# Mixes of a recurrent layer: one fp32 matmul in place of three matmuls of split parts

## The reference

```
xx  = shift(x) - x
xxx = x + xx * time_maa_x
m   = tanh(xxx @ time_maa_w1).reshape(b, t, 4, 32)
m   = einsum('btfd,fdc->fbtc', m, time_maa_w2)      # mw, mk, mv, mr: the four mixes
xw  = x + xx * (time_maa_w + mw)                    # xk, xv, xr alike
r, k, v = xr @ W_r, xk @ W_k, xv @ W_v
w   = time_decay + tanh(xw @ decay_w1) @ decay_w2
y   = wkv6(r, k, v, exp(-exp(w)), faaaa)            # a scan over time for each head
```

## Time and profile before

| what | value |
|---|---|
| median of 3 runs | 2349.08 us (2340.28 to 2349.70) |
| the profiled execution | 2345.97 us, of it 2344.2 us span |
| busy over the span | PE 1941.5 us, DVE 1767.6, POOL 1389.6, ACT 1059.6 |
| time_mix | from 0 to about 1300 us |
| experts and last norm | from about 1300 us to the end |
| granted TensorE clock, mean | 0.924 of full speed |

### The profile page before, as it was taken

One profiled execution on the slowest core, in us unless ns is written; L12 is line 12 of the kernel. 1 busy time (PEld: TensorE's weight loads), 2 busy tenths in 40 slices (PEclk: granted clock), 3 DMA queues, 4 the chain that ended last, 5 costly groups with the idle time before them and its releaser, 6 DMA issues. The chain is left out here.

```text
span 2344.2 us, 35441 instructions
## 1 busy us (share of the span) xinstructions
PE 1941.5 (83%) x11174; PEld 1407.0 (60%) x11174; DVE 1767.6 (75%) x2997; ACT 1059.6 (45%) x1919; POOL 1389.6 (59%) x954
## 2 busy tenths in 40 slices
PE   5777888788777787888765299999999999999980
PEld 2333343334333333333332299999999999999980
DVE  2899999899999999999997266666666666666645
ACT  2233553345334544444433255555555555555546
POOL 3667787768777787677875234444444444444440
PEclk9889999899989989989986599999999999999995
DMA  6832111111112111211020244545444545455438
GB/s 162 220 88 64 47 45 55 46 54 36 53 45 59 28 50 42 60 30 46 31 69 24 66 114 122 121 120 120 120 120 121 121 121 120 118 124 122 119 59 287
DMA packets 172846, 209.03 MB, mean 89 GB/s; under 512 B 12796, under 2 KB 152480, under 8 KB 172768
## 3 DMA queue, kind: packets, MB, share of 16 engines
q1 hardware_dynamic: 112688, 143.09, 20.7%
q0 software_dynamic: 28672, 34.78, 8.6%
q10 hardware_dynamic: 31408, 30.33, 5.0%
HBM read 118.65 MB, written 75.53 MB: 83 GB/s over the span
## 5 line engine op out<-in xcount | busy, mean ns | idle before, releaser
L807 DVE TENSOR_TENSOR_SCAN S<-wT,S,vb 128x512 f32<-128x512 f32 x512 | 624.8, 1262 | 0.0
L1070 POOL TENSOR_TENSOR prod<-S,rT 128x2048 f32<-128x2048 f32 x128 | 536.7, 4198 | 147.9 <-DVE S L807 147.7
L1288 PE MATMUL up<-x_parts,w_parts 128*128 128x308 f32 x3072 | 464.0, 307 | 1.5 <-DVE x_parts L1399 1.5
L1304 PE MATMUL down<-w_parts,h_parts 128*128 128x256 f32 (+1 forms) x3840 | 464.7, 282 | 0.0
L1304 PEld LDWEIGHTS down<-w_parts,h_parts 128*128 128x128 f32 (+1 forms) x3840 | 459.1, 184 | 2.6
L1288 PEld LDWEIGHTS up<-x_parts,w_parts 128*128 128x128 f32 x3072 | 439.2, 189 | 2.1 <-issue 1.8
L1361 POOL TENSOR_TENSOR ye<-ye,weight 128x256 f32<-128x256 f32 (+1 forms) x160 | 210.2, 1314 | 369.6 <-DVE ye L1451 369.6
L1339 ACT ACTIVATE h_full<-up,b_now 128x616 f32<-128x616 f32 x256 | 198.6, 776 | 427.7 <-PE up L1288 426.8
L1369 POOL DMA_INDIRECT sums<-ye,sum_at x160 | 285.0, 1781 | 150.7 <-POOL ye L1361 140.0
L1442 DVE TENSOR_TENSOR h_parts<-h_full,h_parts 128x616 fp32r<-128x616 f32 x256 | 211.4, 826 | 205.5 <-ACT h_parts L1339 205.1
L571 PE MATMUL vb<-v_stack,pick_v 128*128 128x512 f32 x512 | 216.1, 506 | 152.0 <-DVE S L807 151.9
(11 more groups left out here) (173 smaller groups left out, 2454.0 us busy)
## 6 DMA issues: line engine op xcount, KB each, us to landing
w_raw<-in_L_ffn_w_dram SPq DMA_DIRECT2D x64, 1024.0 KB, 8.9
expert_in_rows<-y_tok ACTq DMA_DIRECT2D x30, 652.5 KB, 9.1
xe<-expert_in_rows SPq DMA_DIRECT2D x32, 522.0 KB
v_stack<-v_parts SPq DMA_DIRECT2D x64, 256.0 KB, 4.5
x_tok<-in_L_attn_x_dram SPq DMA_DIRECT2D x16, 512.0 KB, 3.5
x_res<-in_L_attn_x_dram SPq DMA_DIRECT2D x16, 512.0 KB, 3.5
sums<-x_row SPq DMA_DIRECT2D x16, 512.0 KB, 2.9
rows<-sums SPq DMA_DIRECT2D x16, 512.0 KB, 5.5
```

The costliest lines, as they stand in the source:

```text
L807: dve.tensor_tensor_scan(line[:, 1:TC + 1], wT[:, par, half, :], vb[:, p % 2, g, :], line[:, 0:1], ALU.mult, ALU.add).then_inc(scanned, 1)
L1070: pool.tensor_tensor(prod[:, q % 2], S[:, q % RING, :, 0:TC], rT[:, par, half, None, :].to_broadcast([P, QUAD, TC]), ALU.mult).then_inc(pr ...
L1288: last = pe.matmul(up[:, f % 2, half, 0:HC], w1_parts[:, par, wp, k, f * P:(f + 1) * P], x_parts[:, par, xp, k, half * HC:(half + 1) * HC] ...
L1304: last = pe.matmul(down[0:m, (par * TILES + t) % 2, 0:C], h_parts[:, hp, f, t * P:t * P + m], w2_parts[:, par, wp, f, :], start=(f, n) == ...
```

## The change

The row after the tanh stays whole and fp32: ScalarE's tanh (L864) writes `hid` in SBUF and frees the bank; the copy L866 and the subtraction L696 are gone. Each mix is one fp32 matmul of `hid` with `w2_sb`, which holds the unsplit blocks; mw0 waits for the tanh alone. `w2_sb` has half of its columns, its zeroing too, and the four subtractions L667 are gone. Everything else stands in the order in which it stood on every engine.

```diff
-        w2_sb = sb("maa_w2_sb", [P, 2, MIX, C], F32R)
+        w2_sb = sb("maa_w2_sb", [P, MIX, C])
-        hid_parts = sb("hid_parts", [P, 2, TC], F32R)
+        hid = sb("hid", [P, TC])
-        LATER = {"hid": 3, "V": 3, "B": 3}
+        LATER = {"V": 3, "B": 3}
...
-                            for k, (wp, hp) in enumerate(((0, 0), (1, 0), (0, 1))):
-                                if f == 0 and h == 0 and k == 0:
-                                    pe.wait_ge(hid_split, stage_value(i, 1, 1))
-                                if f == 0 and h == 0 and k == 2:
-                                    wait_drained(pe, i, "hid")
-                                last = pe.matmul(pa_of(f"m{n}{h}"), w2_sb[:, wp, f, h * P:(h + 1) * P],
-                                                 hid_parts[:, hp, :], start=k == 0, stop=k == 2)
-                            last.then_inc(a_full, 1)
+                            if f == 0 and h == 0:
+                                wait_drained(pe, i, "hid")
+                            pe.matmul(pa_of(f"m{n}{h}"), w2_sb[:, f, h * P:(h + 1) * P], hid[:],
+                                      start=True, stop=True).then_inc(a_full, 1)
...
-            nc.vector.memset(w2_sb[:].bitcast(F32), 0.0).then_inc(w2_set, 1)
+            nc.vector.memset(w2_sb[:], 0.0).then_inc(w2_set, 1)
...
-            for f, rows in enumerate(blocks):
-                nc.vector.tensor_tensor(w2_sb[rows, 1, f, :], w2_raw[rows], w2_sb[rows, 0, f, :].bitcast(F32),
-                                        ALU.subtract).then_inc(w2_set, 1)
...
-                if s == AT["hid"] + LATER["hid"]:
-                    dve.wait_ge(hid_split, stage_value(i, 1, 1))
-                    dve.tensor_tensor(hid_parts[:, 1, :], pa_of("hid"), hid_parts[:, 0, :].bitcast(F32), ALU.subtract
-                                      ).then_inc(drained_sem("hid"), 1)
...
-                    act.activation(pa_of("hid"), pa_of("hid"), ACT.Tanh).then_inc(hid_set, 1)
-                    act.wait_ge(hid_set, stage_value(i, 1, 1))
-                    act.activation(hid_parts[:, 0, :], pa_of("hid"), ACT.Copy).then_inc(hid_split, 1)
+                    act.activation(hid[:], pa_of("hid"), ACT.Tanh).then_inc(drained_sem("hid"), 1)
```

More of the change, by code:

```diff
@@ L219, in time_mix @@
         v_high = sem("v_high")
-        hid_split = sem("hid_split")
-        hid_set = sem("hid_set")
         v_kept = sem("v_kept")
@@ L438, in _ @@
             pe.wait_ge(own_set, NH)
-            pe.wait_ge(w2_set, 2 * MIX + 1)
+            pe.wait_ge(w2_set, MIX + 1)
             pe.wait_ge(pick_set, 1)
@@ L658, in _ @@
             nc.vector.tensor_tensor(w1_sb[:], w1_sb[:], w1_before[:], ALU.subtract).then_inc(w1_set, 1)
-            nc.vector.memset(w2_sb[:].bitcast(F32), 0.0).then_inc(w2_set, 1)
+            nc.vector.memset(w2_sb[:], 0.0).then_inc(w2_set, 1)
             dve.wait_ge(w2_set, 1)
-            blocks = [slice(f * DMIX, (f + 1) * DMIX) for f in range(MIX)]
-            for f, rows in enumerate(blocks):
-                nc.vector.tensor_copy(w2_sb[rows, 0, f, :], w2_raw[rows]).then_inc(w2_set, 1)
-            dve.wait_ge(w2_set, MIX + 1)
-            for f, rows in enumerate(blocks):
-                nc.vector.tensor_tensor(w2_sb[rows, 1, f, :], w2_raw[rows], w2_sb[rows, 0, f, :].bitcast(F32),
-                                        ALU.subtract).then_inc(w2_set, 1)
+            for f in range(MIX):
+                rows = slice(f * DMIX, (f + 1) * DMIX)
+                nc.vector.tensor_copy(w2_sb[rows, f, :], w2_raw[rows]).then_inc(w2_set, 1)
             nc.vector.tensor_copy(pick_v[:], pick_raw).then_inc(pick_set, 1)
```

## The result

| | before | after |
|---|---|---|
| median | 2347.03 us (2340.28 to 2350.37, 9 runs) | 2356.02 us (2349.93 to 2361.58, 9 runs) |
| profiled execution, its span | 2345.97, 2344.2 us | 2361.58, 2359.9 us |
| VectorE's `keep_now`, first and last chunk | 22.25 and 1132.18 us | 19.40 and 1146.56 us |
| granted TensorE clock, mean | 0.924 | 0.921 |

The ratio is 1.0035, with a 95% interval of 1.0025 to 1.0046: the change costs some 8 us, where 16 to 18 were to be won and the range ended at 2344. The profiled execution of the changed kernel is the slowest of its nine, 5.6 us above their median, so the losses read from it are somewhat larger than the median's.

A forecast was written before the change was run, and what follows sets the result against it. VectorE's queue was taken as the bound in the first stretch. 2.6 (weights) + 15.4 (mw0) - 1.8 (mr) = 16.2 us off 2345.97 gives 2329.8; 2331 us was taken, between that and 2332.9 by the median, range 2318 to 2344.

The forecast's parts named there:

- What bounds the kernel: From 350 to 1250 us VectorE, busy 847.8 of 900 us, sets what the change is worth.
- GpSimd's lag at K0: K0 waits longer for GpSimd, but `vb` behind it has slack: taken as 0, with +2 us as the end.
- Weights ahead of the loop: Half the zeroing (0.85 us) and the four subtractions L667 (1.76 us) leave VectorE's path: 2.6 us won.
- Chunk 0: Ahead of the loop, mw0's gain is given back by the five mixes behind it: 0, ends -0.8 and +1.0 us.
- Ten chunks at mw0: VectorE loses L696 and its wait ahead of mw0's drain: 1.32 us won in each, 13.2 us in all.
- Five late chunks: TensorE comes late to mw0 after slow hid matmuls, so only 0.44 us each is won, 2.2 us in all.
- The price of mr: Each mr mix is ready 0.16 us later, delaying `vb` in nearly every chunk: +1.8 us, ends 0 and 6.3.
- (a): Rival: TensorE is late at mw0 everywhere, the pair running slowly; 2340 to 2343 us. Chance 0.17 with similar ways of losing.
- (b): Rival: later mixes make TensorE stand longer before R and VectorE wait up to 4.10 us a chunk; 2378 us. Chance 0.06.
- (c): Rival: longer mixes fill TensorE's pauses and its clock gains, 26 us won in all; 2320 us. Chance 0.11.
- (d): Rival: an fp32 mix is cheaper or dearer than other fp32 matmuls; no row hints at it, no size or chance given.
- The range: Total time from 2317 us with the best ends to 2346 with the worst; 8 in 10 within 2318 to 2344.

The follow-up runs named there:

- e1_pad: Changed kernel with ten idle semaphore increments on VectorE, four ahead of the loop and six in stage A's copies, restoring the old instruction counts: 2349.11 us.
- e3_pad_early: Changed kernel with both the idle increments of e1_pad and the moved GpSimd multiplication of e2_early: 2341.96 us, ratio 0.9975 to the kernel before.
- e16: The kernel of e5 (changed kernel, four idle increments ahead of VectorE's loop) run again in a later set: 2347.89 us.
- e17: Changed kernel with four idle increments ahead of VectorE's loop and GpSimd's step 3 multiplication put behind step 4's additions, run beside e16: 2339.12 us.
- e6_r410: Kernel before with two float32r matmuls a mix, without subtraction L696 and the four low-weight subtractions (410 and 407 instructions on VectorE): 2336.69 us.
- e5: Changed kernel with four idle semaphore increments on VectorE ahead of its loop, which then begins after 414 instructions in place of 410: 2345.84 us.
- e14_mr_long: Kernel of e12_r_two_early with four float32r matmuls in place of two in each of a chunk's two mr mixes: 2337.78 us.
- e2_early: Changed kernel with GpSimd's multiplication of step 3 put behind the additions of step 4, nothing else: 2351.22 us.
- e12_r_two_early: Kernel before with two float32r matmuls a mix, without subtraction L696, and GpSimd's step 3 multiplication put behind step 4's additions: 2325.24 us.

## Why the prediction was wrong, point by point

- **What bounds the kernel.** VectorE's queue was the right place to look, but it did not bound alone. At K0 GpSimd came within 0.92 us of it, or less, in the trace before; the gain of 1.3 us was larger than that. Its busy share of 690 of 900 us does not show this: from the row sends to K0 it had no pause.
- **GpSimd's lag at K0: the step that failed.** The forecast saw that K0 would wait longer, and took this as 0, with 2 us as the end, since "`vb` behind it has more than a microsecond in hand". That holds where K0 runs fast (at 704.41). Where K0 also ran slowly nothing was in hand, and at 868.41 VectorE stood 1.42 us. Its waits there grew by 7.1 us in all. Measured worth: 7 us between `e1_pad` and `e3_pad_early`, 8.8 between `e16` and `e17`.
- **The loop's return: the step that was missing.** The forecast does not mention VectorE's 2 us at each return, and so put their change at nothing without a reason. They became 3 us through ten fewer instructions, whatever the work (`e6_r410`), and with what hangs on them cost 8 to 10 us in this kernel (`e5`, `e16`). No row of before could give that price; that removing instructions moves the loop could have been named as an open term.
- **Weights ahead of the loop**, 2.6 us: right, 2.85. TensorE's first transpose starts at 19.62 in place of 22.47.
- **Chunk 0**, taken as 0: right. From its `keep_now` to the next chunk's it is 42.1 us, 42.3 before.
- **Ten chunks at mw0**, 1.32 us each: near, at 1.05 in the row shown. The mix itself took 1.15 us for a forecast of 1.14.
- **Five late chunks**, 0.44 us each: wrong in sign, through the return ahead of them. They stood 1.76 to 2.27 us for mw0. With short returns again these chunks take 381.5 us (`e5`, `e16`) and 381.8 before, so 0.3 of the 2.2 us came.
- **The price of mr**, 1.8 us: the size holds at `rstd`, where one wait is 0.99 us for 0.82 and all are 13.7 for 11.8 us, but that place had not been seen. `vb` behind R comes on top, where the wait grew by 3.5 us. `e14_mr_long` shows both places: 0.5 us more per mix cost 12.5 us, or 1.7 times 15 x 0.5. By that factor 0.16 us would cost 4 us, an estimate; the two waits together grew by 5.8 us.
- **Rivals.** (a) holds in the first chunks alone, through the late start; the pair took 1.02 us in all fifteen chunks of the loop, so its rate was never the cause. (b) did not come as it was put: TensorE stood 23.1 us ahead of R in all, 23.3 before. Waits of `vb` grew by 11.6 us, not by 50, and 3.5 of these stand behind R. (c) did not come: the clock in the stretch stayed at 0.91. (d) is out, the mix is an fp32 pair of 1.02 us.
- **The range.** Its worst end was summed wrongly: 2.6 - 1.0 + 4.0 - 6.3 - 2 is a loss of 2.7 us, so 2349 and not "no gain left, 2346". The result lies beyond that too.

The forecast of 2331 us and the result differ by 25: 8 to 10 are the place of the loop, 7 to 9 GpSimd's lag. The 6 to 8 that remain (2337 and 2339 against 2331) fit the longer mixes, mr's 4 to 6 and some 0.3 us of wait at mw0 in the second chunks, but this last sum was only argued, and GpSimd's part is smaller where the loop's place is left as it is (5 us from 2356 to `e2_early`).

## What to carry to other kernels

In this kernel a gain on the engine that bounds was worth little more than the slack of the next engine at the place where they meet. So follow that engine's timeline from its last long piece to the meeting, not its busy share. Where a change removes instructions ahead of or in a rolled loop, compare the waits at the loop's return first, look for instruction packets inside them, and try a few idle instructions ahead of the loop before judging the change. A change that measures as nothing can still be worth its price with one move beside it: here 2356 became 2338 with four idle instructions and one multiplication put later.

## What the runs showed of the hardware

**The return of a loop on VectorE** took 2.0 to 2.4 us with 414 and 407, 418 and 409, or 530 and 407 or 409 instructions ahead of and in the loop, and 2.96 to 3.23 us with 410 and 407, in three kernels with two kinds of mixes. Five of them are 11 or 15 us of VectorE's waits. One packet of instructions starts inside each short return, and two inside each long one.

**TensorE's clock at K0.** The same place of two first chunks of `e5_at414`: windows of 3 us ahead of K0 and from its start, at 463.67 and at 618.58 us.

```profile
460.67:463.67 3.00, 0.61 (x2) 0.48 (x3) 3.00 (x4) 2.71 (x7) 2.92 (x3) 0.98 0.00 0
463.67:466.67 3.00, 3.00 (x5) 1.01 (x3) 3.00 (x5) 0.00 (x0) 2.92 (x3) 0.50 0.00 0
615.58:618.58 3.00, 0.61 (x4) 0.49 (x4) 3.00 (x5) 2.75 (x7) 2.92 (x4) 1.00 0.00 0
618.58:621.58 3.00, 3.00 (x14) 0.93 (x13) 3.00 (x5) 0.60 (x1) 2.92 (x3) 1.00 0.00 0
```

Ahead of both TensorE stood 2.39 us and had the same 0.61 us of work in the window; then K0 ran once at 0.50 of full speed, the 1.2 GHz level (3.52 us for four), and once at 1.00, 2.4 GHz (1.88 us). So the clock fell after this pause once and not the other time: the pause alone does not decide it. K0 was slow in 4 of 15 chunks before, 12 after, 8 and 7 in the two executions of the changed kernel at 414, 2 and 4 in those of the early kernel at 414. In `e12_r_two_early` K0 ran slowly (2.9 to 3.6 us) in four of the five first chunks of an iteration; these took 75.8 to 76.0 us and the fifth 75.3. So much of a slow K0 can be hidden. In the changed kernel VectorE stood about 0.2 us behind a slow K0 for which GpSimd was in time; what the slow stretches cost in all stays open.
